# Two images at a time in the routing of a two-layer attention and mixture-of-experts kernel

## What is computed

```
for layer in (0, 1):
    sa, ca, ga, sb, cb, gb = silu(c) @ wmod            # per image
    h = layernorm(x) * (1 + ca) + sa
    x = x + ga * attention(h)                          # 16 heads of 8; layer 1 adds its own norm and + xn
    h = layernorm(x) * (1 + cb) + sb                   # layer 1: then an RMS norm
    g = h @ Wr                                         # 8 logits for a token
    layer 0: the two best experts, weighted by the softmax of their two logits
    layer 1: the best expert, weighted by its softmax score
    x = x + gb * (weighted sum of the chosen experts of h)
```

## Time and profile before

| what | value |
|---|---|
| runs (three) | 2229.56, 2230.93, 2236.93 us; median 2230.93 |
| profiled execution | 2240.09 us, with a span of 2238.3 us from first to last instruction |
| mean granted clock of TensorE | 0.935 |
| PE busy | 1715.6 us (77% of the span) |
| DVE busy | 1638.5 us (73%) |
| ACT busy | 992.4 us (44%) |
| POOL busy | 884.0 us (39%) |
| executed instructions of all kinds | 53972 |

### The profile page before, as it was taken

The page is one execution under the profiler, slowest core; times in us unless marked ns, Lnnn a source line. Parts: engine busy times, 40 slices in busy tenths (PEclk is TensorE's granted clock), DMA queues, the critical chain, the costliest instruction groups (busy, mean ns, idle before and its releaser), DMA issues. The chain is left out here.

```text
span 2238.3 us, 53972 instructions
## 1 busy us (share of the span) xinstructions
PE 1715.6 (77%) x14370; PEld 1185.4 (53%) x14370; DVE 1638.5 (73%) x5605; ACT 992.4 (44%) x1839; POOL 884.0 (39%) x932
## 2 busy tenths in 40 slices
PE   2588888888888838999935777777877777719997
PEld 1355555555555527989822444444444444417775
DVE  3478888888888845667626888888888888624453
ACT  0265555655555522222212555555555555503322
POOL 0224444444444333444423444444444444203343
PEclk9899999999999968999966999999999999959999
DMA  4334434443434322222235445555455454243332
GB/s 139 49 65 73 69 70 75 70 73 68 74 69 71 64 61 65 67 67 67 66 130 89 91 97 108 102 101 111 96 101 113 94 101 102 56 147 93 93 93 63
DMA packets 267153, 190.44 MB, mean 85 GB/s; under 512 B 26080, under 2 KB 257282, under 8 KB 266326
## 3 DMA queue, kind: packets, MB, share of 16 engines
q1 hardware_dynamic: 251738, 154.75, 35.2%
q0 software_dynamic: 15360, 35.03, 5.3%
HBM read 94.68 MB, written 53.18 MB: 66 GB/s over the span
## 5 line engine op out<-in xcount | busy, mean ns | idle before, releaser
L873 DVE TENSOR_REDUCE mx<-A 128x2 f32<-128x512 f32 x1024 | 685.8, 681 | 147.3 <-PE A L1123 116.1
L728 ACT ACTIVATE probs<-B 128x1024 f32<-128x1024 f32 x512 | 524.4, 1024 | 401.9 <-PE B L1143 211.3
L1123 PE MATMUL A<-stack 126*128 126x256 bf16 x2048 | 397.0, 283 | 168.6 <-DVE mx L873 112.0
L1143 PE MATMUL B<-stack 128*128 128x256 bf16 x2048 | 364.3, 281 | 40.6 <-DMA stack<-mrow 39.2
L1123 PEld LDWEIGHTS A<-stack 126*128 126x128 bf16 x2048 | 159.7, 99 | 343.2 <-DVE mx L873 259.7
L1161 PE MATMUL M<-probs,vals 128*32 128x256 f32 x4096 | 292.8, 404 | 26.5 <-DVE On L896 22.8
L1143 PEld LDWEIGHTS B<-stack 128*128 128x128 bf16 x2048 | 198.5, 102 | 97.7 <-ACT probs L728 26.8
L637 POOL DMA_INDIRECT gathered<-h,slot_in x192 | 187.7, 978 | 155.2 <-DVE slot_in L1017 109.6
L624 POOL TENSOR_TENSOR h<-xn,back_rows 128x256 f32<-128x256 f32 x64 | 46.4, 726 | 487.0 <-DVE xn L828 487.0
L1563 PE MATMUL A<-w2s,hid 128*128 128x128 f32 x1792 | 230.4, 278 | 9.0 <-issue 9.0
L1563 PEld LDWEIGHTS A<-w2s,hid 128*128 128x128 f32 x1792 | 211.8, 192 | 18.4 <-issue 13.4
(11 more groups left out here) (190 smaller groups left out, 2720.6 us busy)
## 6 DMA issues: line engine op xcount, KB each, us to landing
stack<-parts SPq DMA_DIRECT2D x768, 64.0 KB
xt<-gathered SPq DMA_DIRECT2D x112, 132.0 KB, 2.2
probs<-gathered SPq DMA_DIRECT2D x40, 256.0 KB, 2.7
w<-in_w SPq DMA_DIRECT2D x4, 2048.0 KB
back_rows<-mod_rows SPq DMA_DIRECT2D x64, 128.0 KB, 3.4
x_mid<-X SPq DMA_DIRECT2D x64, 128.0 KB, 2.1
Y<-expert_out SPq DMA_DIRECT2D x64, 128.0 KB
X<-in_x SPq DMA_DIRECT2D x32, 128.0 KB, 3.0
```

The costliest lines, as they stand in the source:

```text
L728: act.activation(probs[c % 4][:, :, :, :], Bp[c % 2][:, :, :, :], ACT.Exp, scale=EXP_SCALE[l][c // 4]).then_inc(b_exp.handle, 1)
L873: dve.tensor_reduce(mx[u][:, h, :], A[h % 2][:, :, :], AX.X, ALU.max).then_inc(a_max.handle, 1)
L1123: ins = pe.matmul(A[h % 2][:, t, :], stack[u][0:n, h, 0, t * P:(t + 1) * P], stack[u][0:n, h, 1, :], start=True, stop=True)
L1143: ins = pe.matmul(Bp[c % 2][:, j, t, :], stack[u][:, h, 1, t * P:(t + 1) * P], stack[u][:, h, 0, :], start=True, stop=(l == 1))
```

## The change

It has five parts.

1. `choose_first`, `choose_second`, `weigh_choices`, `place`, `weights` and `count` run once for a pair of images, on four tiles, where they ran once for each image, on two. The choosing is in the tick in which the second image of the pair is at i - 3. Counting, weighing and placing move to the tick after that, in which that image is at i - 4. `read_logits` stays with the image.
2. `count` has five matmuls as before, but for the whole pair: one over 40 columns and four over 32 to 8. `sel` has a fifth, empty tile for the total.
3. `scatter` moves from i - 3 to i - 5, with as many DMAs as before. Of a pair, the first image's scatter is in the tick of its `place`, and the second's in the next tick. `scatter_done` is gone: who needs the buffer waits on the semaphores of the scatter's DMAs. `h2` and `h3` have four buffers.
4. The loop has rounds of four ticks, with 5 rounds for ticks 6 to 25; ticks -3 to 5 and 26 to 36 are written out. Two ticks are added at the end of each attention stage.
5. To make room, `Y` lies in memory of `hid[0]`, which only the expert stages use. One `memset` over all of `h3` and a small one over `sel` replace two over `h3` at the start.

```diff
-        h2 = [sb(f"h2{u}", [P, NT, W]) for u in range(2)]
-        h3 = [sb(f"h3{u}", [P, NT, WX]) for u in range(2)]
+        h2 = sb("h2", [P, HELD, NT, W])
+        h3 = sb("h3", [P, HELD, NT, WX])
...
-        Y = [sb(f"Y{u}", [P, 2, NT, D]) for u in range(2)]
+        Y = [hid[0][:, 2 * u:2 * u + 2, :].rearrange("p c (t d) -> p c t d", t=NT) for u in range(2)]
...
-    for i in range(-DEPTH, DEPTH):
+    for i in range(-LEAD, FIRST):
         tick(peeled(i))
-    pairs = (B - 2 * DEPTH) // 2
+    times = (B - FIRST - LEAD) // UNROLL
...
-    with eng.Fori(0, pairs) as k:
+    with eng.Fori(0, times) as k:
...
+        for i in range(FIRST, FIRST + UNROLL):
+            tick(lambda off, n=2: (k * UNROLL + (i + off), k * (UNROLL // n) + (i + off) // n, (i + off) % n))
...
             def load_gate(b, k, u, q, v):
-                sp.wait_ge(scattered.handle, scattered.after(b - 2))
+                scattered_before(sp, q, v)
...
             def modulate(b, k, u, q, v):
...
-                pool.wait_ge(scattered.handle, scattered.after(b - 2))
+                scattered_before(pool, q, v)
...
-            def scatter_done(b, k, u):
-                pool.wait_ge(scat_out[u], scat_out.of(k))
-                pool.sem_inc(scattered.handle, 1)
...
-                if at(-3):
-                    scatter(*at(-3))
+                if at(-5):
+                    scatter(*held(at, -5))
                 if l and at(3):
                     add_experts(*at(3))
-                if at(-3):
-                    scatter_done(*at(-3))
...
-                step(weights, -3)
+                if group_done(at, -4):
+                    weights(*at(-4))
...
             def residual(b, k, u, q, v):
                 if l:
-                    dve.wait_ge(scattered.handle, scattered.after(b - 2))
+                    scattered_before(dve, q, v)
...
-                layer(0, choose_first, -3)
+                group(0, choose_first, -3)
...
-                layer(0, choose_second, -3)
-                layer(1, choose_first, -3)
+                group(0, choose_second, -3)
+                group(1, choose_first, -3)
...
-                step(weigh_choices, -3)
+                group(l, weigh_choices, -4)
...
-                step(place, -3)
+                group(l, place, -4)
...
-                pe.wait_ge(sel_ready.handle, sel_ready.after(b))
-                pe.matmul(M0[:, PS:PS + E], before_tri[:, :], sel[:, 0, :], start=True, stop=True)
...
+                pe.wait_ge(sel_ready.handle, sel_ready.after(k))
+                pe.matmul(M0[:, PS:PS + (GT + 1) * E], before_tri[:, :], sel[:, :, :].rearrange("p t e -> p (t e)"),
+                          start=True, stop=False)
+                for n in range(1, GT + 1):
+                    ins = pe.matmul(M0[:, PS + n * E:PS + (GT + 1) * E], ones_b[:, :],
+                                    sel[:, 0:GT + 1 - n, :].rearrange("p t e -> p (t e)"), start=False, stop=(n == GT))
+                ins.then_inc(pos.handle, 1)
...
-                if at(-3):
-                    m0_read(*[(x1_ready, -2)] * (l == 0), (base_ready if l else v_ready, 0), (mT_read, -1, 2))
-                    count(*at(-3))
+                if group_done(at, -4):
+                    m0_read(*[(x1_ready, -2)] * (l == 0), (base_ready if l else v_ready, 0), (logits_read, -3))
+                    count(*at(-4))
```

## The result

Nine runs of each on the same chips: 2241.76 us median (2239.61 to 2247.9) for the changed kernel, 2232.93 us (2227.01 to 2237.37) for the kernel before. The ratio is 1.0043 (95% interval 1.0031 to 1.0054): the change costs about 9 us where I had forecast a gain of 41.

What follows compares the result with a forecast made beforehand. Neither DVE nor PE alone bounds attention ticks: PE nearly covers DVE in layer 0, DVE holds PE back in layer 1. The sum -53.7 + 7.6 + 5 = -41 us gives 2190 us from 2230.93; range 2160 to 2222.

Steps and rivals of the forecast that it cites:

- half of the chain: Attention ticks: one routing chain in two ticks saves 0.9 us a tick in layer 0, 0.95 in layer 1; 53.7 us.
- the longer loop: Attention stages' loop: jumps back over four ticks may wait for instruction loads; 5 us taken, between zero and 18.
- The window without a chain: Trace before image 0 is chosen: ticks without routing are 1.36 us shorter in layer 0, 1.74 in layer 1.
- my 0.2 us for counting: Allowance per attention tick for counting, also missing from the window, leaving 1.15 and 1.5 us for the whole chain.
- my own sign that the halves don't find room: Attention ticks in the profile after: unlike lengths by turns, over 1 us apart, would show it.
- bound by PE all the same: Rival, 17%: attention ticks stay set by PE and its hand-overs; gain 0.3 and 0.5 us a tick, about 2220 us.
- The relief of DVE itself: DVE in attention ticks: relieved by 1.95 us a tick in layer 0 and 1.08 in layer 1, 88 us in all.
- instructions of twice the width: Chain on DVE: 32 values for 16, about 1 ns a value, so 10 to 20 ns more each.
- code that no longer stays resident: Rival, 9%: each round of four ticks reloads code, 10 us a round, 100 us over 10 rounds, about 2285 us.
- the 4.6 us a round from which I had it decide: Attention loop: reload cost per round that would use up the 46 us of gain left over 10 rounds.
- The ends: Ends of the attention stages: one image more scattered after the last `place`, 5.1 us in layer 0, 2.5 in layer 1; +7.6.
- POOL's wait: POOL's split in attention ticks: no longer held up to 3.03 us by `scatter_done`; no separate gain counted.

Runs made afterwards that it cites:

- before_all_written_out: The kernel before, with no loop in the attention stages, every engine's ticks written out: 2197.11 us, ratio 0.9827 to the kernel before.
- after_all_written_out: The changed kernel with no loop in the attention stages, every engine's ticks written out: 2184.9 us, ratio 0.9787 to the kernel before.
- the doubled choosing: The changed kernel, all written out, with `first_of` done twice in each choosing tick: 2241.28 us, ratio 1.004 to the kernel before.
- before_rounds_of_four: The kernel before, still routing each image by itself, with loop rounds of four ticks in place of two: 2267.43 us, ratio 1.0147.
- after_one_image: The changed kernel, all written out, with GROUP = 1 (each image routed by itself in one tick), scatter kept at i - 5: 2218.25 us, ratio 0.9928.
- after_one_image_scatter_at_once: The changed kernel, all written out, each image routed by itself, scatter back at i - 3: 2193.69 us, ratio 0.982 to the kernel before.
- after_spread_end: The changed kernel, all written out, last pairs counted and placed a tick early, last scatters dealt out over ticks 32 to 34: 2185.21 us, 0.9788.

## Why the prediction was wrong

Of the 50 us between the forecast and the measurement, two terms of the sum have 46: the 53.7 us for half of the chain, of which 22 came, and the 5 us for the longer loop, of which at least 19 came.

**The window without a chain.** I compared it with ticks of the loop, 21.10 against 22.46 us, and gave the difference of 1.36 us to the chain. But that window lies in the part that is written out, and the others don't. In before_all_written_out the same window is 20.88 us, and the 26 ticks of the earlier trace rows are 21.91 us each (170.05 to 739.73 us): the whole chain costs 1.03 us, with counting. In layer 1 the window is 21.63 us and the 26 ticks are 23.04 us each (1267.28 to 1866.18): 1.41 us in place of my 1.74. A tick in the loop costs 0.55 us over the same tick written out in layer 0 (22.46 - 21.91) and 0.70 in layer 1 (23.74 - 23.04). Not all of that was in my price, since the windows themselves, written out in both kernels, read 0.2 and 0.4 us shorter here. So this fault is worth a third of a microsecond in each layer.

**What half of the chain is worth: the step that failed.** Forecast 0.9 and 0.95 us a tick, 53.7 us in all. Measured between the two kernels written out: 673.8 - 662.1 = 11.7 us in layer 0 and 702.7 - 692.2 = 10.5 in layer 1, 22 us, or 0.4 us a tick. The window alone doesn't explain it. With my 0.2 us for counting taken off, it should have read 0.83 and 1.21 us, and with the shares that I took (0.9 of 1.15, and 0.95 of 1.5) that would still have been about 41 us, by my estimate. The larger fault is the share: I took nearly all of the chain's cost for half of the chain, since DVE had 4.6 us to spare. What came is half of it in layer 0 and under a third in layer 1. In layer 1 the ticks with a pair's choosing stayed near the 23.0 us of a tick with a whole chain, and only the ticks without it got shorter (22.9 and 22.0 us on average; the granted clock is mostly 0.92 or 0.93 in the longer ones and 1.00 in the shorter). That comes close to my own sign that the halves don't find room, ticks over 1 us apart by turns. The case that I called bound by PE all the same had 0.3 and 0.5, 23 us in all, and that sum is what came, with the layers the other way round. The relief of DVE itself was right (80 us for 88), as were instructions of twice the width (0.19 us where they took 0.17). One count was wrong and did no harm: the chain of layer 0 has 24 DVE instructions beside `read_logits`, not 21 (the change takes away 5605 - 4981 = 624 of them, 16 times 24 + 15). Its 4.1 us were read from the timeline and stand.

DVE's time does not carry over: where it is relieved, DVE waits for PE (166.6 us for A in after_all_written_out, 108.3 in before_all_written_out). What the sum lacked, as I read it, is that the price depends on the lump. The chain's lumps of 1.15 and 1.41 us lay almost under cover, since PE has two A buffers; the doubled choosing had 2 us more in a tick and paid 56 us for 59. That a lump of pairs is itself no longer than one of a single image but for 0.02 us an instruction would then be why pairs win at all. Only the doubled choosing tests this; no run makes the lumps shorter or takes an A buffer away.

**The loop.** Forecast 5 us, with 0 and 18 as bounds; measured 57 us for rounds of four against 38 for rounds of two, 19 us net, just outside. The run that changes nothing but the length of the round, before_rounds_of_four, puts it higher, at 34 us. The mechanism that I gave 9%, code that no longer stays resident, is there. It did not turn the sign alone: with my 5 us in place of 19 the sum put right below is a gain of 10 us, and with my 53.7 us in place of 22 it is a gain of 28. Nor did it reach, on average, the 4.6 us a round from which I had it decide. The eight long ticks exceed their neighbours by 2.8 to 5.5 us each, 4.1 on average, about 33 us in all (18.8 in layer 0 over neighbours of 21.9, 14.1 in layer 1 over 23.5). I had priced a round at 10 us, over twice too much, and ten rounds where there are eight jumps back; and I had not seen that PE's clock falls with the pause. What I had taken as evidence, 55 loads in the whole run, showed rightly that two ticks stay resident, and says nothing of four. The second step that failed is the 5 us in the sum: taken between zero and one DMA's landing a jump, without a price for what PE does after an idle stretch. The Trainium skill, "Runtime: NRT & Kernel Launch", section "Instruction fetch mechanics", has a jump out of what the queue of instructions holds stall for a DMA. The trace agrees: eight pauses right behind the eight jumps back, 2.9 us each, each with a load in it, and no load in the rounds of the kernel before. They come with DVE's loop alone and with the longer round alone. What stays open is the pause's length: in the second one the profile has the load's packets on the DMA engines for only 0.4 us of 2.79, and no view shows what fills the rest.

**The ends.** Forecast 7.6 us, 5.1 in layer 0. Measured 8.3 us between the stages with loops and 11.0 without, and about nothing or a gain behind layer 1 (309.4 for 310.8). I counted the scatters behind the last `place`, eight for four. The pile behind the last `modulate` was missing: sixteen, since images 28 and 29 are scattered only then. I also held the move of the scatter for free because POOL has time; after_one_image shows that its place in the tick isn't free, by 14 us in layer 1. With pairs this is mostly not seen (L972 and L902 at 295 and 184 ns in after_all_written_out).

**POOL's wait.** Gone, and with it PE's wait for the stacked parts in layer 0, as forecast: 22.8 us from 150 to 700 us, and not one after. The 28.1 us above lie at the starts of the stages (21.0 before 150 us, 5.8 from 1150 to 1240). I had counted no gain from it. What it brought at most is the 4.8 us of layer 0 between before_all_written_out (673.8) and after_one_image_scatter_at_once (669.0). That is net of a cost that I had not seen: the earlier split now meets the chain in nearly every tick of layer 0, and the first comparison of the choice takes 0.91 us on average in after_one_image_scatter_at_once for 0.42 in before_all_written_out.

**The sum put right**, between the medians, where before has 2232.93: with the loop at 19 in place of 5, half of the chain at 22 in place of 53.7, and the ends at 7 net (11.0 and -4.0 in the account) in place of 7.6, it is +4 us, for a measured +9. The rest, 5 us, is about what separates single profiled executions (the two written out differ by 17 us in span and by 12 in medians), and I leave it open. The other way round, over the kernel before with rounds of four, the medians alone close it: +34 us for the round, -26 for everything else.

What stays open too: where in a tick of a two-tick loop its 0.5 us lie. The 6328 instructions more that it executes (122 for each of 52 looped ticks, over five engines) are there, but no run here took them apart. The end of layer 0's stage with pairs, 63.4 us from the last mark to the release when the scatters are dealt out, is 8.7 us over the 54.7 of the kernel before written out, and the two timelines account for it: 5.0 us are the four scatters more behind the last place; 2.6 are the last `modulate`, which stands behind eight scatters in a row and begins 39.0 us after the last mark and not 36.4; 0.8 is the longer way from the last scatter to the release, and 0.3 lies between `modulate` and the last place.

The best of these kernels is after_all_written_out, at 0.9787 of the kernel before (after_spread_end is level with it): pairs and no loop. Of its 48 us, 38 come from the loop's going in the kernel before, and about 10 (12 between the medians) from the rest of the change. That is the pairs net of what the later scatter costs.

## What to carry to other kernels

A window of the trace that lacks the work in question is a good way to price it only if all else is alike, and whether it is looped or written out is part of that. When a change makes a loop's body longer, look first at whether the code still stays resident: ask the trace for loads of instructions inside the rounds, count pauses on "issue" once for each round right behind the jump back, and price the slower clock of PE behind such a pause with it. On an engine that trades two buffers with another, don't take the relief of that engine for a gain in time: here 80 us of relief were worth 22, while 59 us more in one place cost 56. And moving an instruction of POOL to another part of the tick can cost DVE more than POOL gains.

## What the runs showed of the hardware that was not expected

- A jump back over four ticks of DVE's code: 2.9 us of standstill on average in the changed kernel (23.4 us in 8), 3.2 in before_rounds_of_four (25.4 in 8) and 4.0 with all others written out (31.8 in 8), against at most 0.3 us for a jump over two ticks. Every pause of the changed kernel has one load of instructions of q14 in it, and the rounds of two ticks have none. PE stood still 4.8 us at one of its eight jumps back.
- Around such a point, where PE idled for 2.75 us, its granted clock was 0.50 for some 7 us by the windows of 2 us, and 16 matmuls took 1.94 us for 1.07.
- Even a loop whose jumps show no pause costs: 22.46 us for a tick that takes 21.91 written out.
- Two DVE instructions (a two-input one, and a scaling by a column) that met POOL's `add_experts` ended when its instructions ended: 0.63 and 0.70 us for 0.16 and 0.29. In layer 0 it strikes the chain itself: comparing the logits with their maximum takes 1.02 us on average over 13 instructions in after_all_written_out (140 to 700 us), while the same comparison of the second choice takes 0.19. One of them, 422.80 to 423.82 us, ends as POOL's split L627 ends (423.77). The Trainium skill, "SBUF — State Buffer", section "Who interferes with whom", has a DVE instruction with two inputs in SBUF and a GpSimd instruction that reads SBUF exclude each other, and names `tensor_scalar` as a form that can take the shared ports as well; the trace agrees on both.
